# Second cross-attention: the output bank is emptied by a ScalarE copy, the reciprocal is cut in four, the maxima start one chunk earlier

## What is computed

```
x = x + tanh(g_xattn[0]) * L0_xattn(layernorm(x), ctx, mask)   # softmax over 1601 tokens
x = x + tanh(g_ffn[0])   * L0_ffn(layernorm(x))                # Hadamard, 8-bit, ternary weights
x = x + tanh(g_xattn[1]) * L1_xattn(layernorm(x), ctx)         # this change
x = x + tanh(g_ffn[1])   * L1_ffn(layernorm(x))                # NF4 weights, SwiGLU

def L1_xattn(qkv, y):            # qkv: (4, 512, 512), y: (4, 1601, 512); 16 heads
    ch = 512 // 16                                    # 32 channels per head
    q = qkv.reshape(4 * 16, ch, 512)                  # tokens are the channel axis here
    k = v = y.reshape(4 * 16, ch, 1601)
    weight = softmax(einsum('bct,bcs->bts', q, k) / sqrt(ch))
    return einsum('bts,bcs->bct', weight, v)
```

## Time and profile before

| | us |
|---|---|
| median of 3 executions | 2000.08 (1994.62 to 2001.67) |
| the profiled execution | 1990.66 |
| its span in the trace | 1988.8 |
| TensorE busy | 1719.1 (86%) |
| VectorE busy | 1290.5 (65%) |
| ScalarE busy | 777.5 (39%) |
| GpSimd busy | 829.1 (42%) |

### The profile page before, as it was taken

How to read it: one execution, slowest core, us unless ns; L and a number is a source line. 1 busy time by engine, 2 the same in 40 slices (tenths; PEclk the granted TensorE clock), 3 DMA queues, 4 the chain that set the end, 5 groups by cost and what they waited for, 6 DMA issues and landing times. The chain is left out here.

```text
span 1988.8 us, 23904 instructions
## 1 busy us (share of the span) xinstructions
PE 1719.1 (86%) x8103; PEld 871.0 (44%) x8134; DVE 1290.5 (65%) x1649; ACT 777.5 (39%) x1275; POOL 829.1 (42%) x369
## 2 busy tenths in 40 slices
PE   5999999994656777899999998999999986989996
PEld 2444444442444543444444444444444323444443
DVE  3668989857898775766666665666666413565553
ACT  1211212113444533565655555655565554011010
POOL 0012222012554426577776676777767660000000
PEclk9999999996788876999999998999999996999999
DMA  8030312302000045143344444443332302000002
GB/s 320 9 114 20 89 44 66 124 34 82 1 0 0 0 104 142 39 105 92 87 98 105 105 105 106 105 94 78 89 86 70 71 1 87 1 0 0 0 0 85
DMA packets 83551, 137.19 MB, mean 69 GB/s; under 512 B 16606, under 2 KB 53490, under 8 KB 82678
## 3 DMA queue, kind: packets, MB, share of 16 engines
q1 hardware_dynamic: 83446, 135.84, 25.0%
HBM read 70.73 MB, written 8.66 MB: 40 GB/s over the span
## 5 line engine op out<-in xcount | busy, mean ns | idle before, releaser
L1257 DVE TENSOR_REDUCE c_piece_max<-c_unit 128x1 f32<-128x804 f32 x512 | 484.2, 990 | 280.4 <-PE c_unit L1383 277.1
L1342 ACT ACTIVATE c_prob<-c_scores 128x512 f32<-128x512 f32 (+1 forms) x832 | 472.2, 596 | 365.6 <-PE c_scores L1400 356.4
L1192 POOL TENSOR_TENSOR c_prob_sum<-c_prob_sum,c_prob 128x2048 f32<-128x2048 f32 x96 | 439.7, 4580 | 68.3 <-ACT c_prob L1342 64.3
L1400 PE MATMUL c_scores<-c_queries,c_keys 98*128 98x512 f32 (+1 forms) x832 | 358.1, 451 | 30.9 <-ACT c_prob L1342 16.6
L1383 PE MATMUL c_unit<-c_khigh,c_qdiag 128*128 128x402 f32 x1024 | 315.0, 393 | 23.3 <-DVE c_piece_max L1257 12.5
L1383 PEld LDWEIGHTS c_unit<-c_khigh,c_qdiag 128*128 128x128 f32 x1024 | 189.0, 204 | 175.9 <-DVE c_piece_max L1257 92.3
L1409 PE MATMUL c_out<-c_prob,c_VT 128*32 128x512 f32 (+1 forms) x1664 | 228.4, 629 | 22.1 <-issue 22.1
L1400 PEld LDWEIGHTS c_scores<-c_queries,c_keys 98*128 98x128 f32 (+1 forms) x832 | 158.0, 193 | 186.6 <-ACT c_prob L1342 132.3
L525 PE MATMUL a_S<-a_ctxT,a_xnT 128*128 128x401 f32 x512 | 188.9, 513 | 7.2 <-ACT a_prob L490 3.9
L555 PE MATMUL a_o<-a_ctx,a_probT 128*128 128x512 f32 (+1 forms) x416 | 181.2, 592 | 0.0
L1192 POOL TENSOR_TENSOR c_prob_sum<-c_prob 128x2048 f32<-128x2048 f32 x16 | 72.5, 4534 | 137.0 <-ACT c_prob L1342 137.0
(11 more groups left out here) (204 smaller groups left out, 2099.1 us busy)
## 6 DMA issues: line engine op xcount, KB each, us to landing
c_keys<-c_khigh SPq DMA_DIRECT2D x128, 200.2 KB, 3.0
c_k<-in_keys SPq DMA_DIRECT2D x16, 801.0 KB, 6.3
c_keys<-c_k SPq DMA_DIRECT2D x64, 200.2 KB, 3.0
a_ctx<-in_ctx SPq DMA_DIRECT2D x12, 1024.0 KB, 5.4
c_VT<-in_values SPq DMA_DIRECT2D x16, 768.0 KB
a_ctxT<-in_ctxT SPq DMA_DIRECT2D x12, 802.0 KB, 4.8
c_queries<-c_qhigh SPq DMA_DIRECT2D x128, 64.0 KB, 2.6
a_weights<-in_L_ffn_weight SPq DMA_DIRECT2D x3, 1408.0 KB, 13.6
```

Source lines behind the costliest of these rows:

```text
L1192: nc.gpsimd.tensor_tensor(psum4[:], a[:], prob[(j * MC + c) % RING][:], ALU.add).then_inc(sums_taken, 2 if i == 1 else 1)
L1257: nc.vector.tensor_reduce(piece_max[j % 2][:, k // 2, k % 2:k % 2 + 1], U[bank(unit)][:, :, 0:PIECE], axis=AX.XY, op=ALU.max).then_inc(uni ...
L1342: nc.scalar.activation(prob[(j * MC + c) % RING][0:w, h, :], STp[h % 2][0:w, :], ACT.Exp, scale=SCALE).then_inc(exp_done, 1)
L1400: nc.tensor.matmul(STp[h % 2][0:w, :], K[p][:, h, c * P:c * P + w].bitcast(F32R), Q[p][:, h, :].bitcast(F32R), start=True, stop=True).then ...
```

## The change

In `cross_attention_1`, besides a small part elsewhere (a third identity tile, `ident_f16`, which nothing uses, and its two GpSimd instructions go):

- `take_out` on ScalarE copies `c_out` times the gate to a new SBUF tile `c_out_taken`, between the second and the third exponential of chunk 0 of the next group. TensorE's first `out` waits for that copy (`out_taken`) instead of `gain_ready`.
- `finish` on VectorE is the reciprocal alone, in four parts of 128 columns, ahead of units 0, 2, 4 and 6 of the slot. TensorE waits for all parts (`rden_ready`) before it writes `c_den` anew, at chunk 4.
- `add_gain` on GpSimd waits for both, multiplies `c_out_taken` by the reciprocal, and adds the product to `x`: one instruction more, in the same place.
- `first_gap` is 0 instead of 4: the units are spread over all 52 gaps.

```diff
-            def finish(g):
-                steps = Steps(dve, fin_steps, g, FINS)
-                dve.wait_ge(den_done, g + 1)
-                wait(dve, x_added, g)
-                steps.link(nc.vector.reciprocal(rden[:], DEN[:]))
-                dve.wait_ge(pv_done, PV0 + (g + 1) * CHUNKS)
-                nc.vector.scalar_tensor_tensor(rden[:], O[:], gates[:, 1:2], rden[:], ALU.mult, ALU.mult).then_inc(gain_ready, 1)
-                steps.close()
+            def finish(g, i):
+                cols = slice(i * D // PARTS, (i + 1) * D // PARTS)
+                if i == 0:
+                    dve.wait_ge(den_done, g + 1)
+                    wait(dve, gain_ready, g)
+                nc.vector.reciprocal(rden[:, cols], DEN[:, cols]).then_inc(rden_ready, 1)
...
+                for u, unit in enumerate(stream):
+                    if before and u % 2 == 0 and u // 2 < PARTS:
+                        finish(g - 1, u // 2)
...
             def add_gain(g):
+                pool.wait_ge(out_taken, g + 1)
+                pool.wait_ge(rden_ready, PARTS * (g + 1))
+                nc.gpsimd.tensor_tensor(taken[:], taken[:], rden[:], ALU.mult).then_inc(gain_ready, 1)
                 pool.wait_ge(gain_ready, g + 1)
-                pool.wait_ge(consts_ready, 3)
                 x = X[:, bass.ds(g, 1), :].rearrange("p o d -> p (o d)")
-                nc.gpsimd.tensor_tensor(x, x, rden[:], ALU.add).then_inc(x_added, 1)
+                nc.gpsimd.tensor_tensor(x, x, taken[:], ALU.add).then_inc(x_added, 1)
...
+            def take_out(g):
+                act.wait_ge(pv_done, PV0 + (g + 1) * CHUNKS)
+                wait(act, x_added, g)
+                nc.scalar.activation(taken[:], O[:], ACT.Copy, scale=gates[:, 1:2]).then_inc(out_taken, 1)
+
             def exponentials(g, j, c):
                 w = P if c < MC - 1 else ML
                 for h in range(H):
+                    if c == 0 and h == 2 and (not isinstance(g, int) or g > 0):
+                        take_out(g - 1)
...
-                    wait(pe, gain_ready, g)
+                    wait(pe, out_taken, g)
...
             def den(g, j, c):
                 k = ML if c == MC - 1 else P
+                if c == SUMMED[0]:
+                    wait(pe, rden_ready, PARTS * g)
...
-                first_gap, gaps = 4, H * MC
+                first_gap, gaps = 0, H * MC
```

More of the change, by code:

```diff
@@ L1008, in cross_attention_1 @@
         rden = sb("c_rden", [P, D])
+        taken = sb("c_out_taken", [P, D])
         U = [ps(f"c_unit{j}", [P, 2, 512]) for j in range(2)]
@@ L1036, in cross_attention_1 @@
         sums_taken = sem("c_sums_taken")
+        rden_ready = sem("c_rden_ready")
+        out_taken = sem("c_out_taken")
         gain_ready = sem("c_gain_ready")
@@ L1039, in cross_attention_1 @@
         stat_steps = sem("c_stat_steps")
-        fin_steps = sem("c_fin_steps")
-        FINS = 1
+        PARTS = 4
         STACKS, ROWS, DIAGS = 16 * H * 6, 16 * H, 16 * H
@@ L1283, in slot @@
             def slot(g, j, main, nxt, more, later):
-                if main and (not isinstance(g, int) or g > 0):
-                    finish(g - 1)
-                for unit in unit_stream(g, j, main, nxt, more):
+                before = main and (not isinstance(g, int) or g > 0)
+                stream = unit_stream(g, j, main, nxt, more)
+                if before and not stream:
+                    for i in range(PARTS):
+                        finish(g - 1, i)
+                for u, unit in enumerate(stream):
+                    if before and u % 2 == 0 and u // 2 < PARTS:
+                        finish(g - 1, u // 2)
                     if later and unit[2:] == (j + 2, 0):
@@ L1301, in _ @@
             every_slot(dve, slot)
-            finish(G - 1)
-            dve.wait_ge(gain_ready, G)
+            for i in range(PARTS):
+                finish(G - 1, i)
+            dve.wait_ge(rden_ready, PARTS * G)
         @block.scalar
@@ L1365, in _ @@
             every_slot(act, slot)
+            take_out(G - 1)
         @block.tensor
@@ L1707, in program @@
         ident_bf = stack.enter_context(nc.sbuf_tensor("ident_bf", [P, P], BF16))
-        ident_f16 = stack.enter_context(nc.sbuf_tensor("ident_f16", [P, P], F16))
         gates = stack.enter_context(nc.sbuf_tensor("gates", [P, 4], F32))
@@ L1716, in program @@
             sem(n) for n in ("gates_loaded", "gates_ready", "ident_ready", "ident_steps", "weights_stored", "stored"))
-        shared = dict(X=X, ident=ident, ident_bf=ident_bf, ident_f16=ident_f16, gates=gates, gates_ready=gates_ready, ident_ready=ident_ready,
+        shared = dict(X=X, ident=ident, ident_bf=ident_bf, gates=gates, gates_ready=gates_ready, ident_ready=ident_ready,
                       weights_stored=weights_stored)
@@ L1734, in _ @@
                 steps = Steps(pool, id_steps)
-                for eye in (ident, ident_bf, ident_f16):
+                for eye in (ident, ident_bf):
                     steps.did(pool.memset(eye[:], 0.0))
                 steps.settle()
-                for eye in (ident, ident_bf, ident_f16):
+                for eye in (ident, ident_bf):
                     steps.did(pool.affine_select(out=eye[:], in_=eye[:], compare_op=ALU.not_equal, fill=1.0, base=0,
```

## The result

The changed kernel took 1944.17 us, the median of 4 executions (1940.25 to 1953.13), against 2000.88 for the kernel before in the same comparison: a ratio of 0.9726, 95% interval 0.9684 to 0.9768. The forecast was 1954.6, in a range from 1938 to 1981. The profiled execution is the slowest of the four, 1953.13, with a span of 1951.3.

The account below looks back on a forecast made before the run. The prediction took TensorE, 86% busy, as the bound, through its work, waits and clock. Fourteen slots at -3.18 us gave -44.5, with -2 and +1.0 made -45.5: 1945.2 profiled, 1954.6 as median, range 1938 to 1981.

Parts of the forecast that it names:

- The wait and the copy: Slot start: TensorE's wait for `c_out` goes, -1.58 us per slot; ScalarE's copy delays exponentials, +0.2 (bounds 0 and +0.7).
- So nothing waits there: -22.1 us in all: First output of each group on TensorE: bank free before TensorE arrives, so all the wait goes, -1.58 per slot.
- another wait lies under the one removed: Rival at the first output: it also waits for values and chunk 0's exponentials; about 1995 us, chance 0.06.
- The clock: TensorE's clock over the 14 slots: expected to stay at 2.4 GHz, -1.3 us per slot (bounds 0 and -1.9).
- the forecast left 3 to it: Slot at the loop's turn, 57.7 us: 3 us of it left to the loop when estimating the clock's excess.
- both of the forecast's reasons: Why TensorE's clock should stay at 2.4 GHz: the wait gone, and three units put in the thin stretch ahead.
- the clock still falls: Rival: TensorE's clock still falls once a slot, giving 18.2 us back; 1972.8 us, chance 0.17.
- Reciprocal in four and spread: VectorE's parts between maxima delay units in chunk 1, +0.2 per slot; units spread over all gaps, -0.7.
- the 0.76 it had: Chunks 3 to 12: two units fewer behind outputs, 0.38 us each, taken as -0.7 per slot.
- GpSimd: Multiplication on GpSimd: chunk 3's sum ends 3.1 us later, ring slack 0.4 remains; cost 0 (bounds 0 and +1.5).
- Group 0 and the end: Once each: group 0's slot with four units in the formerly empty chunk 1, -2 us; tail after group 15, +1.0.
- The slower rival: Reciprocal part costs nearly the whole's 3.35 us, so TensorE waits on unit banks; +70, 2070 us, chance 0.04.

Follow-up runs that it names:

- copy_alone: The changed kernel with the reciprocal in one part and first_gap back at 4, leaving ScalarE's copy and GpSimd's multiplication; 1966.77 us, ratio 0.9867.
- late_units: The changed kernel with first_gap back at 4, so copy and four reciprocal parts without the spread of units; 2005.43 us, ratio 1.0049.
- one_part: The changed kernel with one reciprocal of 512 columns instead of four parts, so copy and spread stay; 1996.44 us, ratio 1.0010.
- wait_two_parts: The changed kernel, where the first output of a group also waits for the second part of the reciprocal; 1953.68 us, ratio 0.9798.
- pool_more: The changed kernel with two more 128 x 512 multiplications on GpSimd ahead of its addition; 1966.35 us, ratio 0.9844.

## Why the prediction was right, by its steps

The kernels with and without each part (no copy in the first row; us per mean slot, ratio of the total):

| | units late | units spread |
|---|---|---|
| no copy, one reciprocal | 54.16 | 55.47 (1.0096) |
| copy, one reciprocal | 52.11 (0.9867) | 54.05 (1.0010) |
| copy, four parts | 54.56 (1.0049) | 50.62 (0.9726) |

The parts do not add up. Beside the copy, the spread alone costs 1.94 and the parts alone 2.45; together they give 1.49. Each removes what the other brings: the spread needs its banks before a reciprocal of 3.35 us is over, and the parts need early units to come early themselves.

*The wait and the copy*: forecast -1.58 + 0.2. The copy was priced rightly: it delays the exponentials by 0.19. The wait was not: copy_alone shows -0.9 for both at the full clock. "So nothing waits there: -22.1 us in all" is the step that was too large. With the output 1.55 earlier, the score behind it waits 0.40 for ScalarE, whose work on the queries had been hidden under the wait. The rival "another wait lies under the one removed" was right in kind and small in size.

The Trainium skill (ScalarE: Activation LUTs, What ACT_TABLE_LOAD costs) gives 93 ns for a pointer operand; the trace agrees, 0.69 for the copy with its gate as scale against 0.59 for a plain copy.

*The clock*: forecast -1.3. By the same mark the mean slot stood 54.16 - 52.60 = 1.56 above the full-clock slot and stands 50.62 - 50.28 = 0.34 above it now: -1.22. What is left is the slot at the loop's turn, 5.4 above the others at a clock of 0.94, where it was 5.3 above before; the forecast left 3 to it. The clock was lowered somewhere in 11 of the 13 other slots before, in 6 with the copy alone, in 5 with copy and parts (late_units), in 10 with copy and spread but a bank wait of 2.56 (one_part), and in none in the changed kernel, nor with its wait of 0.65 to 0.88 (wait_two_parts). So both of the forecast's reasons bear on it: without the long wait the clock falls in fewer slots, and with chunk 1 filled as well it falls in none. How a wait that begins after the fall, as in the earlier trace rows, adds to the count stays open. The rival "the clock still falls" was half right for the copy alone. The Trainium skill (TensorE: Matmul & The Clock Gate, A second HAM failure mode: psum-queue depth-cycling) says that frequent short idling between groups of matmuls can make the clock oscillate. The trace of copy_alone agrees, with gaps of 0.20 to 0.28 ahead of that output; the changed kernel does not, whose chunk 1 has gaps of 0.16 to 0.27 among its units at a clock of 1.00.

*Reciprocal in four and spread*: forecast +0.2 - 0.7 = -0.5. At the full clock, 51.70 to 50.28, they gave -1.4. A part takes 0.94 (forecast 0.95), and the bank waits are 3.9 us over 13 slots, 0.3 each (forecast 0.2). What was mis-sized is the spread, by 0.9. Where the time went is seen in the chunks, from the starts of their first scores in PE's timeline, mean of the slots of groups 2 to 13 that kept the full clock throughout (6 and 11 of them), with the number of units in each:

```
             0    1    2    3    4    5    6    7    8    9    10   11
copy_alone  5.70 2.45 3.81 4.97 3.11 4.45 3.35 3.46 4.50 3.60 3.33 4.98
  units     3    0    3    3    2    3    3    2    3    3    2    3
after       5.48 3.01 3.19 4.19 3.46 4.22 3.47 3.35 4.32 3.60 3.47 4.52
  units     3    3    2    3    2    3    2    3    2    3    1    3
```

Chunks 1 and 2 together take 6.26 with three units and 6.20 with five, so the two units more there are free, as the forecast said. Chunks 3 to 11 give 1.15, with two units fewer. In copy_alone, as in the kernel before, a unit waits 0.25 for its bank in chunk 3 and again in chunk 11 (6.3 us in 25 waits from 882 to 1590); after, all 13 such waits lie in chunk 1. These 0.50 are a term the forecast did not have, and by their size 0.65 remain for the two units, near the 0.76 it had. The 0.22 of chunk 0 stays open.

*GpSimd*: forecast 0, with 0.4 of slack left. The slack is 0.41; pool_more and late_units show what lies behind it.

*Group 0 and the end*: forecast -2 and +1. Group 0's slot went from 65.0 to 64.8: chunk 10 in it grew from 4.63 to 6.72, with a wait of 1.06 for a unit bank and an output at the lower clock behind it. Group 15's slot went from 43.4 to 45.8, with the clock at 0.89 instead of 0.96. Together they cost 2.2, where -1 was forecast.

*Sum*: per slot, -0.9 for wait and copy (forecast -1.38), -1.42 for parts and spread (forecast -0.5) and -1.22 for the clock (forecast -1.3) are -3.54, against -3.18. The 14 slots gave 49.5 (forecast 44.5), the two ends took 2.2 back, and the stage gave 47.3 (forecast 45.5). The forecast came out close because errors cancelled: a wait counted too high and two ends too good against a spread counted too low. That the profiled execution took 1953.1, and not the 1945.2 forecast for it, lies in `ffn_1`. *The slower rival*, a part that costs like the whole, falls with its 0.94. *Another wait underneath* is the 0.40 above.

Between the profiled executions `ffn_1` moved by 10.5 us with its clock. Why was not tried.

## What to carry to other kernels

A wait that is taken away is worth its length only as far as no other engine has used it to catch up: look at when each engine would be ready behind it. A copy put into an engine's idle time is free only for the part that passes before its next input is there. Measure slots from one event on the same engine in both kernels. Where a long operation is cut up among others, the last piece's time depends on where those others stand: count who waits for it, and how much slack is left there. And test parts of such a change together as well as one by one: here the copy alone gave 1.3%, the spread alone lost 1.0%, the copy with either of the other two gave nothing or lost 0.5%, and all together gave 2.7%.

## What the runs showed of the hardware

The granted clock of TensorE fell behind a stretch that had no gap over 0.3 us but thin work, which I had not expected (copy_alone); gaps of 0.65 to 0.88 in a dense stretch left it at 1.00 (wait_two_parts). A reciprocal of 128 columns takes 0.94 and one of 512 takes 3.35, as the line through 1 and 512 columns said. The slot at the turn of the loop takes 5.4 us more than the others when these run at the full clock; its own clock is 0.94, so a part of that is the clock.
